# Second convolution of a graph network on one Trainium2 core: the tail of a finished block of nodes (ELU, third product, node shifts) runs two blocks behind the sums instead of one

## The reference

```python
h = jnp.maximum(_layernorm(x, axis=-1), 0.0)
h1 = elu(spline_conv(ones, row, col, basis, idx, stn1_w, stn1_b))       # [N, 64]
h2 = elu(spline_conv(h1,   row, col, basis, idx, stn2_w, stn2_b))       # [N, 64]
h3 = elu(h2 @ stn3_w + stn3_b)                                          # [N, 64]
t  = h3 @ stn4_w + stn4_b                                               # [N, 3], the node shifts
new_pseudo = clip(pseudo + t[col] - t[row], 0, 1)
x = x + spline_conv(h, row, col, basis2, idx2, conv_w, conv_b)          # third convolution
# spline_conv: out[i] = mean over edges of i of  sum_s basis_s * x[col] @ W[idx_s], + b;  W is [125, Fin, Fout]
```

## Time and profile before

| | |
|---|---|
| median of 3 runs | 13772.33 us (13738.16 to 13816.77) |
| span of the profiled execution | 13681.2 us |
| what lies between that span and the median | 91.1 us |
| busy: PE, DVE, ACT, POOL | 7155.1, 7727.2, 2965.5, 7334.9 us |
| mean granted TensorE clock | 0.698 of full speed |

### The profile page before, as it was taken

One profiled execution on the slowest core, in us unless ns is written; L12 is line 12 of the kernel. 1 busy time (PEld: TensorE's weight loads), 2 busy tenths in 40 slices (PEclk: granted clock), 3 DMA queues, 4 the chain that ended last, 5 costly groups with the idle time before them and its releaser, 6 DMA issues. The chain is left out here.

```text
span 13681.2 us, 203231 instructions
## 1 busy us (share of the span) xinstructions
PE 7155.1 (52%) x48670; PEld 6010.6 (44%) x48670; DVE 7727.2 (56%) x17337; ACT 2965.5 (22%) x9191; POOL 7334.9 (54%) x7456
## 2 busy tenths in 40 slices
PE   3466666664765777777899455555555500000000
PEld 2355555553664566555688444344455400000000
DVE  9744444443775445444577444343367546777777
ACT  0011111111222233222344222222234200010001
POOL 4256555552004888888400678777700066666663
PEclk9866666666887888888999656565588655555555
DMA  1200000006223333333322233232222211112121
GB/s 38 86 2 2 2 2 2 2 2 9 31 31 70 77 79 81 75 77 76 70 57 57 46 49 49 45 48 46 48 44 42 28 41 48 52 49 53 49 53 43
DMA packets 1774339, 603.40 MB, mean 44 GB/s; under 512 B 1584837, under 2 KB 1715365, under 8 KB 1774050
## 3 DMA queue, kind: packets, MB, share of 16 engines
q1 hardware_dynamic: 1062354, 307.85, 11.2%
q0 software_dynamic: 255648, 274.30, 9.8%
q10 hardware_dynamic: 456304, 20.89, 2.8%
HBM read 429.15 MB, written 172.95 MB: 44 GB/s over the span
## 5 line engine op out<-in xcount | busy, mean ns | idle before, releaser
L1187 PE MATMUL c_acc<-c_spread_sb,c_basis_sb 128*125 128x256 f32 (+1 forms) x12544 | 2813.1, 388 | 1026.1 <-issue 422.0
L1187 PEld LDWEIGHTS c_acc<-c_spread_sb,c_basis_sb 128*125 128x125 f32 x12544 | 2331.1, 234 | 1420.1 <-issue 722.1
L1554 POOL DMA_INDIRECT at_ring<-gat_table,at_place x1568 | 1583.9, 1010 | 1478.5 <-issue 1478.5
L606 POOL DMA_INDIRECT rec<-rk_rec,rk_place x1568 | 1615.2, 1030 | 1108.8 <-DVE rk_place L496 617.8
L942 POOL DMA_INDIRECT c_ring<-hid_table,c_at x1568 | 1638.8, 1045 | 478.7 <-issue 457.8
L942 POOL DMA_INDIRECT c_ring<-feat_table,c_at x1568 | 1562.7, 997 | 477.8 <-issue 464.1
L1061 DVE TENSOR_TENSOR c_spread_sb<-c_mark,c_rin 128x512 f32<-128x512 f32 (+1 forms) x3136 | 1745.3, 557 | 53.8
L1273 ACT ACTIVATE c_sums<-c_acc 125x512 f32<-125x512 f32 (+1 forms) x3136 | 1446.4, 489 | 1499.1 <-PE c_acc L1187 1135.8
L1201 PE MATMUL c_mix<-c_sums,c_w 125*64 125x128 f32 (+1 forms) x18816 | 1292.3, 304 | 539.7 <-issue 411.6
L1201 PEld LDWEIGHTS c_mix<-c_sums,c_w 125*64 125x64 f32 (+1 forms) x18816 | 1006.8, 140 | 828.6 <-issue 655.3
L1811 PE MATMUL gr_hps<-ident,gr_hs 128*32 128x128 f32 x98 | 29.9, 409 | 2469.5 <-issue 1907.8
(11 more groups left out here) (357 smaller groups left out, 10706.8 us busy)
## 6 DMA issues: line engine op xcount, KB each, us to landing
c_rin<-rows SPq DMA_DIRECT2D x3136, 42.0 KB
c_rin<-rows SPq DMA_DIRECT2D x3136, 20.0 KB
rows<-c_ring POOLq DMA_DIRECT2D x392, 128.0 KB
rows<-rk_blank SPq DMA_DIRECT2D x112, 252.0 KB
rows<-c_ring POOLq DMA_DIRECT2D x392, 72.0 KB
rows<-at_ring SPq DMA_DIRECT2D x196, 144.0 KB
rec<-rk_rec,rk_place POOLq DMA_INDIRECT x1568
c_ring<-hid_table,c_at POOLq DMA_INDIRECT x1568
```

Of the source, the lines that this page charges most:

```text
L606: pool.indirect_dma_start(out=d.rec, out_offset=bass.IndirectOffsetOnAxis(ap=place[:, u, j:j + 1], axis=0), in_=rec[:, u, j, :], in_offset ...
L1187: last = pe.matmul(acc[pp % BANKS][:, (w % 2) * WN * feats:(w % 2 + 1) * WN * feats], basis[:, q, w, :, :].rearrange("p a b -> p (a b)"), ...
L1554: pool.indirect_dma_start(out=ring[:, u, j, :], out_offset=None, in_=d.gat_table, in_offset=bass.IndirectOffsetOnAxis(ap=place[:, u, j:j + ...
```

## The change

The tail of a block runs two blocks behind the sums, and its three steps on DVE stand at other places. `earlier(f, b, item, n)` calls a step for block `b - n`, and nothing while there is none. On DVE, `scale` of block b-2 comes before the first half of block b, `hide` of block b-2 before the second half, and `deepen` of block b-3 behind the second spread of the first half. On PE, transpose and third product of block b-2 stand in the first half (behind pieces 2 and 5) instead of the second (pieces 2 and 4), the shifts of block b-2 at the block's end. On ACT, `lift` of block b-1 stands behind piece 12, the copy of the transpose behind piece 3, the second ELU behind piece 7. The number of steps is the same; the first blocks are written out (three instead of one), and behind the loop more steps are left over. SP, POOL and the third convolution keep their order.

```diff
+    head = 3 if moved is None else 1
+    def earlier(f, b, item, n):
+        if moved is None and not (isinstance(b, int) and b < n):
+            f(b - n, item - n)
...
-                if at == (0, 3):
-                    dve.wait_ge(added, item + 2)
-                    dve.scalar_tensor_tensor(v1[:, :], conv_out[:, bass.ds(k, 1), :].rearrange("p b o -> p (b o)"),
+            def scale(k, item):
+                dve.wait_ge(added, item + 2)
+                dve.scalar_tensor_tensor(v1[:, :], conv_out[:, bass.ds(k, 1), :].rearrange("p b o -> p (b o)"),
...
-                            follow(b - 1, item - 1, (q, k))
+                        if (q, k) == (0, 1):
+                            earlier(deepen, b, item, 3)
...
                 dve.wait_ge(summed, m * pieces + pieces)
+                earlier(hide if q else scale, b, item, 2)
...
-                for k in range(2 * pieces):
-                    follow(NB - 1, o * NB + NB - 1, divmod(k, pieces))
+                for f, back_by in ((deepen, 3), (scale, 2), (hide, 2), (deepen, 2), (scale, 1), (hide, 1), (deepen, 1)):
+                    earlier(f, NB, o * NB + NB, back_by)
...
+            def turn(k, item):
+                pe.wait_ge(b_hidden, item + 1)
+                pe.wait_ge(b_rowed, item * 3 + 1)
+                pe.wait_ge(b_copied, item + 1)
...
-                            follow(item - 1, b - 1, (q, w // 2))
+                        if (q, w // 2) == (0, 2):
+                            earlier(turn, b, item, 2)
+                        elif (q, w // 2) == (0, 5):
+                            earlier(third, b, item, 2)
...
+                    earlier(shift, b, o * NB + b, 2)
...
-                            follow(b - 1, item - 1, (q, pp - q * pieces))
+                        if pp == 3:
+                            earlier(copy_turned, b, item, 2)
+                        elif pp == 7:
+                            earlier(lift_deep, b, item, 2)
+                        elif pp == 12:
+                            earlier(lift, b, item, 1)
...
-                        follow(b - 1, o * NB + b - 1, (2, 0))
+                    earlier(store_rows, b, o * NB + b, 2)
```

More of the change, by code:

```diff
@@ L1213, in _, with block_of @@
             with pe.Fori(0, n) as o:
-                for q in range(2):
-                    body(0, o * NB, q)
-                after(0, o * NB)
-                with pe.Fori(1, NB) as b:
+                def block_of(b):
                     for q in range(2):
@@ L1220, in _ @@
                     after(b, o * NB + b)
-                    follow(o * NB + b - 1, b - 1, (2, 0))
-                for k in range(2 * pieces + 1):
-                    follow(o * NB + NB - 1, NB - 1, divmod(k, pieces))
+                    earlier(shift, b, o * NB + b, 2)
+                for b in range(head):
+                    block_of(b)
+                with pe.Fori(head, NB) as b:
+                    block_of(b)
+                for back_by in (2, 1):
+                    for f in (turn, third, shift):
+                        earlier(f, NB, o * NB + NB, back_by)
         @block.scalar
@@ new lines, in lift, with copy_turned @@
+            def lift(k, item):
+                act.wait_ge(b_scaled, item + 1)
+                act.activation(under1[:, :], v1[:, :], ACT.Relu, scale=-1.0).then_inc(b_bent, 1)
+                act.activation(over1[:, :], v1[:, :], ACT.Relu).then_inc(b_lifted, 1)
+                act.wait_ge(b_bent, item + 1)
+                act.activation(fall1[:, :], under1[:, :], ACT.Exp, scale=-1.0).then_inc(b_lifted, 1)
+            def copy_turned(k, item):
+                act.wait_ge(b_turned, item + 2)
+                act.activation(hid2_t[:, :], turn_ps[0:HID, 0:P], ACT.Copy).then_inc(b_copied, 1)
@@ new lines, in store_rows @@
+            def store_rows(k, item):
+                act.wait_ge(b_stored, item * 32 + 32)
+                act.activation(row[:, 0:FEAT], c.h[:, bass.ds(k, 1), :].rearrange("p b f -> p (b f)"), ACT.Copy)\
+                    .then_inc(b_rowed, 1)
+                act.wait_ge(b_moved, item + 2)
+                act.activation(row[:, FEAT:FEAT + 3], turn_ps[:, 2 * P:2 * P + 3], ACT.Copy).then_inc(b_rowed, 1)
+                act.activation(step[:, 0:3], turn_ps[:, 2 * P:2 * P + 3], ACT.Copy).then_inc(b_rowed, 1)
+                act.wait_ge(b_rowed, item * 3 + 4)
+                rows = bass.ds(k * P, P)
+                act.dma_start(d.feat_table[rows, :], row[:, :]).then_inc(b_stored, 16)
+                act.dma_start(d.move[rows, :], step[:, :]).then_inc(b_stored, 16)
@@ L1302, in block_of @@
                     take_block(b)
-                    if not (isinstance(b, int) and b == 0):
-                        follow(b - 1, o * NB + b - 1, (2, 0))
+                    earlier(store_rows, b, o * NB + b, 2)
                 make_sides(0, 0)
-                block_of(0)
-                with act.Fori(1, NB - 1) as b:
+                for b in range(head):
+                    block_of(b)
+                with act.Fori(head, NB - 1) as b:
                     block_of(b)
                 block_of(NB - 1)
-                for k in range(2 * pieces + 1):
-                    follow(NB - 1, o * NB + NB - 1, divmod(k, pieces))
+                for f, back_by in ((copy_turned, 2), (lift_deep, 2), (lift, 1), (store_rows, 2),
+                                   (copy_turned, 1), (lift_deep, 1), (store_rows, 1)):
+                    earlier(f, NB, o * NB + NB, back_by)
             if moved is None:
```

103 lines of the change are left out of this document (34 added, 69 removed).

## The result

The changed kernel takes 13812.17 us, the median of 20 runs (13750.07 to 13897.42), against 13726.67 us for the kernel before (20 runs, 13611.38 to 13838.19). The ratio is 1.0068, 95% interval 1.0049 to 1.0088: slower by 0.7%, where the forecast was no change. Three later reruns beside the kernel before, on two chips, gave 1.0062 (1.0025 to 1.0098), 1.0061 (1.0035 to 1.0087) and 1.0051 (1.0019 to 1.0084).

The account below looks back on a forecast made before the run. PE was taken to set the pace, with DVE's stop costing it 0.42 us a block after the gathers. Terms -14.7 and +4 gave -11 us: 13761 us from 13772, called no change, range 13630 to 13850 (8 in 10).

Parts of the forecast that it names:

- Part 1: DVE's stop at `mt_v` goes, so PE gets its spread in time: 0.42 us a block after the gathers, -14.7 us.
- Part 1, second half: Same DVE stop in the 62 gather blocks: saving bounded by 1.2 us in all, taken as 0.
- part 4: ACT's ELU waits for `scale` (T+7.5; T starts a block's sums), reached about T+12.9; margin 5 us: 0.
- Part 2: SP's window loads move earlier along with the spreads; nothing on the path, hidden by PE: 0.
- Part 3: PE's transpose and third product move to the first half, none added: between -10 and +20 us, taken as 0.
- Part 5: At the end, the tail of the block before joins the last block's: bounds 0 and 7.2, taken as +4 us.
- The paragraph on what could be large: Gather blocks' unexplained excess in product and handover, 682 us; left in place, but what runs beside it changes.
- B: Rival, slower: window loads beside whole product and gap slow PE; +170 us, half 13846; mark: product over 15 us; chance 0.14.
- A: Rival, faster: with DVE and SP at work the gather blocks' handover shortens; -170 us, 13590; chance 0.2.
- C: Rival: freed DVE held elsewhere, `lift`, transpose or `mt_hid` waiting for a late step; +49 us, 13810; chance 0.06.
- D: Rival: DVE stays behind and the 1.28 us between copies stay; +4 us, 13776; chance 0.05.

Follow-up runs that it names:

- c1: Kernel before, with the second convolution's window loads waiting until all its gathers are done: 14678.42 us.
- c2: Changed kernel, with the second convolution's window loads waiting until all its gathers are done: 14607.53 us.
- e8: Changed kernel plus 16 unused DVE products a block in blocks 3 to 59, scaling behind the fourth: 0.9880 of before, slow kind of chip.
- r3: Changed kernel with PE's and ACT's small steps back in the second half and `mt_hid3` later on DVE: 1.0030 of before, slow kind of chip.
- e7: Changed kernel plus 22 unused DVE products a block in blocks 3 to 47, scaling behind the tenth: 0.9913 of before, slow kind of chip.
- the held ones: Changed kernel with DVE waiting for the block before, as before the change: 1.0114 and 1.0110 of before on the fast kind of chip, 1.0102 on the slow.
- r2: Kernel before, unaltered, on the slow kind of chip: ratio 1, the base, with 38.8 us a gather block.
- e9: Changed kernel plus five POOL semaphore increments behind each gather: 1.0201 of before, slow kind of chip.
- r7: Changed kernel with DVE waiting for the block before, as before the change: 1.0102 of before, slow kind of chip.
- e5: Changed kernel plus 26 unused DVE products a block in blocks 3 to 47, all before the scaling: 1.0118 of before, fast kind of chip.
- r8: Changed kernel, unaltered, on the slow kind of chip: 1.0051 of before.
- r5: Kernel before, unaltered, on the fast kind of chip: ratio 1, the base, with 34.6 us a gather block.

## Why the prediction was wrong, point by point

- **The number.** 13812 us lies inside the range of 8 in 10 (13630 to 13850), by luck: the three runs that it was built on had the kernel before at 13772, twenty put it at 13727. The sign was wrong, and so was "no change": the interval of the ratio begins at 1.0049.
- **Part 1, right.** 0.42 us a block after the gathers was forecast, 0.47 measured; c1 and c2 show it in all blocks once no gather runs. Two of its signs were ill chosen: `mt_v` still has idle time before it (258.3 us from 6625 to 7745, off the path), and the step from the last copy of the first half to the first of the second is 1.19 us (6984.95 to 6986.14), because ACT's second ELU now stands there.
- **Part 1, second half: the step that failed.** "In the 62 gather blocks the saving is bounded by 1.2 us in all: 0." The saving was; the cost wasn't looked for. "DVE is idle 923.9 us here, and it costs PE nothing" was read as: where DVE is idle doesn't matter. It does, as far as e8's two sorts of block show. The change moved that idle time from the end of the product and the handover, where one completion is waited for, into the first half of the sums, where ACT waits for eight and PE has four banks. A gather block took 45.4 us instead of 38.6 in the profiled execution, 6.8 more: sums +4.0, product +2.7, wait before back -0.9, the third product's own idle time +1.3 (74.7 us in 50 blocks against 14.7 in 61), with a lower granted clock. In the reruns it was 42.2 to 44.4 us against 38.8: sums +3.5 to +4.2, product +0.4 to +1.9, wait -1.3 to -1.7. So the 0 of the gather blocks was some 4 us a block in the sums. The sums' part is tied to the late completions; why the product lengthens, mostly in PE's own records and in gaps without a wait, stays open. In part 4 "ACT is there at about T+12.9" held only where completions come at once.
- **Part 2, not refuted.** The loads moved; no run put a cost on them.
- **Part 3, its reasons right, its bound too small.** After the gathers it cost nothing. In them the third product waits for ACT's copy 45.3 us in 22 waits, above the 20 us allowed; r3 puts what their place cost at 0.3% at the most likely (1.0062 against 1.0030, intervals that overlap).
- **Part 5, right.** From the last `hid` to the last store it was 7.4 us (7574.33 to 7581.77) and is 10.65 (7744.56 to 7755.21), +3.2 where +4 was taken:

```profile
7744.56 0.22 ACT L1305 ACTIVATE hid<-c_back 128x64 f32<-128x64 f32 x1 [0.53 <-PE c_back L1220]
...
7755.21 0.46 ACTq L1273 DMA_DIRECT2D move<-mt_step  x1
```

- **The rivals.** The paragraph on what could be large named the right place, and B the right sign: 85.5 us came, about its half. Its mark, a product of over 15 us, was met in the profile (16.6) and in two of three reruns (14.8, 15.1, 16.3); its mechanism, the loads, found no support, and most of the loss lay in the sums. A named a real effect as well: the wait at the handover did get shorter (5.0 to 4.1 us, and 1.8 in e7). C did not occur in the changed kernel (ACT never waits for `mt_v`), only in the held ones. D fell: PE's wait for a spread is gone.
- **The pages cited.** Letting the loads run ahead shows no cost on the product (12.9 us in r3 against 14.4 in r2). This doesn't contradict what the Trainium skill, "SBUF — State Buffer", section "SBUF: two separate sides", says of DMA and compute, and doesn't prove it either. That matmul ends are estimated ("Perfetto Trace Analysis", section "Tensor Engine Instruction (MATMUL, LD_WEIGHTS)", also of the Trainium skill) limits what is read here: the lateness is counted from modelled ends. The prediction put the 6 us down to products still under way, which no freed DVE can shorten. The lateness did get shorter in the blocks in which DVE worked (e8, 2.7 to 0.6 us a piece). Whether what is late is the matmul itself or only the report of its end, these traces don't tell.

So the prediction also had its chances wrong: it names 682 us of unexplained excess in the stretch that the change rearranges, and gives two thirds to nothing happening to it.

**Open.** Why PE's completions come forward while DVE works, why the blocks of e7 without extra work are short, and what the product's gaps are. In the product of after shown above PE's records come in ones, twos and threes every 0.7 us for 9 us, with no semaphore to wait for, so late completions can't be all that slows PE beside the gathers:

```profile
5613.64 0.38 PE L1212 MATMUL c_mix<-c_sums,c_w 125*64 125x128 f32 x2 [0.20 <-issue]
5614.36 0.27 PE L1212 MATMUL c_mix<-c_sums,c_w 125*64 125x128 f32 x1 [0.35 <-issue]
5615.09 0.34 PE L1212 MATMUL c_mix<-c_sums,c_w 125*64 125x128 f32 x2 [0.46 <-issue]
```

In the slow kind's runs the mean gather instruction on POOL goes the other way as the block: 1008 ns in after, 1046 in before, 1090 in e7, 1069 in e8, 1006 in e9; r7 with 1043 doesn't fit. That is company, not proof. Open too is what makes a chip of either kind, and whether the changed kernel loses on the fast kind at all: it wasn't timed there. Blocks 49 to 65 of e5, which have the changed kernel's order, took 33.1 us each there by their first pieces, less than before's 34.6.

## What to carry to other kernels

An engine's idle time that "costs nothing" may still go with a cost by when it falls: if another engine's completions are late in a stretch, ask which waits the change moves under that lateness, and how many of them there are a round. When an excess in the stretch is unexplained, its size belongs in the range of any change that rearranges the stretch. And look at the buffers between producer and consumer where completions are late: with four banks PE's sums ran without idle time when a copy came 0.1 us late (c2), and lost 2.6 us a block at 2.6 us (after). More banks were not tried.

## What the runs showed of the hardware

- While POOL issues indirect gathers, PE's completion comes long after the modelled end of its matmul: 6.2 us at the handover in the earlier trace rows, 5.2 us on average from 4500 to 5900 in before; without gathers ACT starts within 0.05 us at the handover of c1. Two engines that wait for the same completion are released together, 0.17 us apart, however late it is.
- Unused vector work on constants, with its semaphore counts, made the changed kernel 1.2% faster than before and 1.7% faster than itself without it (e8 and r8, 0.9880 against 1.0051), and unused semaphore increments on POOL, which cost POOL nothing visible, made it 1.5% slower (1.0201 against 1.0051).
- Two kinds of chip, some 4.5% apart in this program. It doesn't lie in the gathers: before's took 2475 us from first to last on a fast one (r5) and 2458 on a slow one, and 2302 where no block ran beside them (c1).
- In the three handovers shown above the granted clock is 0.50 to 0.64 of full speed, while PE works 2.0 to 2.3 of 3.8 to 7.5 us. The first pieces behind a handover can run slowly too: at 5499.47 in after 12 records take 4.54 us, with a granted clock of 0.59 over the first 3.78 us, against 2.85 us for the 12 at 5508.13, where it is 1.00.

```profile
5499.47 4.54 PE L1196 MATMUL c_acc<-c_spread_sb,c_basis_sb 128*125 128x256 f32 x12
```
